# A convolution kernel in fp32: GpSimd's products released by their pixels alone, and three steps of the start in another order

## What is computed

```python
t1 = p1_w * x                          # a factor per channel and row
t2 = x + t1
t4 = relu(x)
t5 = unfold(x, 3, 7)                   # the 21 taps of a 3 x 7 window
t7 = einsum('oc,nchw->nohw', p7_w, t4)
t8 = unfold(t7, 1, 5, dilation 3)      # five columns, three apart
t9 = x[:, :, None] - t8
t10 = einsum('ngihw,goi->ngohw', t2 in 4 groups, p10_w in 4 groups)
t11 = einsum('nck,nmk->ncm', t1, t5) / sqrt(h * w)
t12 = t9.mean(2)
t13 = einsum('ncm,nmk->nck', t11, t10) / sqrt(c * 21)
out = maximum(t13, t12)
```

## Time and profile before

| what | value |
|---|---|
| time, median of 3 runs | 389.67 us (389.62 to 389.78) |
| the profiled execution | 390.18 us |
| its span, first to last instruction | 388.4 us |
| mean granted clock of TensorE, as a share of 2.4 GHz | 0.999 |
| TensorE busy with matmuls | 381.5 us |
| VectorE busy | 328.2 us |
| ScalarE busy | 254.2 us |
| GpSimd busy | 88.7 us |
| data moved by DMA | 88.8 MB, mean 229 GB/s |

### The profile page before, as it was taken

The page is one execution under the profiler, slowest core; times in us unless marked ns, Lnnn a source line. Parts: engine busy times, 40 slices in busy tenths (PEclk is TensorE's granted clock), DMA queues, the critical chain, the costliest instruction groups (busy, mean ns, idle before and its releaser), DMA issues.

```text
span 388.4 us, 10235 instructions
## 1 busy us (share of the span) xinstructions
PE 381.5 (98%) x4024; PEld 169.4 (44%) x4024; DVE 328.2 (85%) x401; ACT 254.2 (65%) x721; POOL 88.7 (23%) x77
## 2 busy tenths in 40 slices
PE   6999999999999999999999999999999999999996
PEld 3233563334733356333643338333383334732383
DVE  7898999899798896888968887888868889688645
ACT  2535379779577664677466772776827768377790
POOL 1635212221232202222022220222202222222300
PEclk9999999999999999999999999999999999999999
DMA  7999486483977656784677937779377673553115
GB/s 281 388 350 410 181 283 210 167 303 114 328 268 258 212 199 218 257 308 147 215 223 259 337 112 248 232 265 322 120 250 249 246 283 111 174 181 111 54 57 216
DMA packets 28704, 88.80 MB, mean 229 GB/s; under 512 B 3312, under 2 KB 3824, under 8 KB 28656
## 3 DMA queue, kind: packets, MB, share of 16 engines
q1 hardware_dynamic: 28656, 88.14, 65.0%
HBM read 71.35 MB, written 16.78 MB: 227 GB/s over the span
## 4 chain that ended last, share of the span: by engine, by line
PE 98%; issue 1%; DVE 0%; DVEq 0%
PE ps_y L828 43%; PE ps_y L927 13%; PE ps_t L850 12%; PE ps_p L850 12%; PE ps_y L839 9%; PE ps_t L927 2%; PE ps_y L850 1%; PE ps_y L1072 1%; PE ps_p L1010 1%; PE ps_t L828 1%; PE ps_y L975 1%; PE ps_p L828 1%; PE ps_p L975 0%; PE ps_t L1010 0%; PE ps_t L839 0%
## 5 line engine op out<-in xcount | busy, mean ns | idle before, releaser
L828 PE MATMUL ps_y<-v_planes,u_planes 64*64 64x512 f32 x1488 | 183.4, 594 | 2.0 <-issue 1.8
L306 POOL TENSOR_TENSOR t1T<-t1T,p1T_sb 128x512 f32<-128x512 f32 x64 | 81.2, 1292 | 267.8 <-PE ps_y L839 237.0
L414 ACT ACTIVATE t<-xn,p_plus 128x64 f32<-128x64 f32 x512 | 127.9, 334 | 0.0
L850 PE MATMUL ps_t<-t,aT 64*64 64x512 f32 x440 | 113.0, 590 | 0.1
L850 PE MATMUL ps_p<-box,p_fifth 64*64 64x512 f32 x424 | 108.8, 589 | 0.0
L828 PEld LDWEIGHTS ps_y<-v_planes,u_planes 64*64 64x64 f32 x1488 | 54.9, 133 | 112.9 <-issue 107.9
L641 DVE STREAM_TRANSPOSE yT<-ps_y 128x512 f32<-128x512 f32 x62 | 40.7, 695 | 30.3 <-PE ps_y L839 29.9
L338 ACT ACTIVATE base<-ps_p 128x512 f32<-128x512 f32 x55 | 32.8, 597 | 47.4 <-PE ps_p L850 46.9
L927 PEld LDWEIGHTS ps_y<-t1T,yT 128*128 128x128 f32 x448 | 50.5, 192 | 5.7 <-issue 5.7
L927 PE MATMUL ps_y<-t1T,yT 128*128 128x128 f32 x448 | 51.9, 277 | 0.0
L675 DVE TENSOR_TENSOR base<-ps_t,base 128x512 f32<-128x512 f32 x56 | 38.5, 687 | 12.0 <-PE ps_t L850 11.8
(11 more groups left out here) (75 smaller groups left out, 219.1 us busy)
## 6 DMA issues: line engine op xcount, KB each, us to landing
xw<-x_conv SPq DMA_DIRECT2D x63, 561.0 KB, 6.6
xn<-x_nat SPq DMA_DIRECT2D x32, 512.0 KB, 4.5
t1T<-x_pix SPq DMA_DIRECT2D x32, 512.0 KB, 5.1
out<-base SPq DMA_DIRECT2D x63, 256.0 KB, 4.7
u_planes<-w_tiles SPq DMA_DIRECT2D x4, 336.0 KB, 6.4
out<-base SPq DMA_DIRECT2D x2, 128.0 KB, 2.1
p1T_sb<-p1T SPq DMA_DIRECT2D x1, 128.0 KB, 7.4
p_sb<-p7T SPq DMA_DIRECT2D x1, 64.0 KB, 7.7
```

The lines of the kernel that those rows point to most:

```text
L306: nc.gpsimd.tensor_tensor(part, part, p1T_sb[:, e, :].unsqueeze(1).broadcast_to([P, 4, C]), ALU.mult).then_inc(t1_ready, 1)
L414: last = nc.scalar.activation(t2[:, h, W * r:W * (r + 1)], xn[:, f, at:at + W], ACT.Copy, scale=p1_plus[:, 8 * h + r:8 * h + r + 1])
L828: last = nc.tensor.matmul(dst[TILE * pair:TILE * pair + TILE, :], weights_of(rows_of(half), u, weights, TILE * k, TILE), data_of(rows_of(h ...
L850: last = nc.tensor.matmul(dst[cols, 0:data.shape[-1]], weights[rows, cols], data[rows, :], start=start, stop=False, skip_group_check=True)
```

## The change

It has three parts.

GpSimd's parts of t1 no longer wait for `m_done` in images 1 to 7. What stays is the wait for the quarter of pixels that they read. Image 0 keeps both.

In the start, x of group 5 (the sixth) is loaded ahead of quarters 2 and 3 of image 0's pixels and of the second natural tile.

Also in the start, VectorE does `box_pairs(0, 0)` ahead of the planes of group 5 instead of behind `seeds(4)`, and ScalarE does `t2_half(0, 1)` behind two `seed_x` instead of ahead of `copy_two(4)`.

```diff
             load_group(4)
+            load_group(5)
             load_pixels(0, 2, 4)
             load_natural(0, 1)
-            load_group(5)
             load_natural(0, 2)
...
             for n in range(1, N_IMG):
-
                 for q in range(8):
-                    pool.wait_ge(m_done, GROUPS * n + 1 + q // 2)
                     t1_part(n, q)
...
             relu(0, 1)
-            t2_half(0, 1)
 
             copy_two(4)
             seed_x(0, 0)
             seed_x(0, 1)
+            t2_half(0, 1)
...
             seeds(3)
+            box_pairs(0, 0)
             planes_low(5)
             planes_high(5)
             turn_y(2)
 
             seeds(4)
-            box_sums(0, 0)
+            box_fours(0, 0)
+            box_last(0, 0)
```

## The result

The changed kernel takes 413.47 us in the median, against 389.7: the ratio is 1.0596, 95% interval 1.0569 to 1.0623, so 23.8 us slower. Six executions lie between 410.18 and 417.14 us; those of before agree within 0.2 us. The ratio is taken without the slowest one, 417.14, which lies over 1.5% above the fastest. The profiled execution took 412.30 us, its span is 410.5.

The account below looks back on a forecast made before the run. TensorE, busy 381.5 of 388.4 us, was taken as the bound. Images 2 to 7 lose 13.5 and image 1 4.8, the start and tail 0: 18.3 us on 389.67 gives 408.0 us, range 391 to 420.

Parts of the forecast that it names:

- narrower range: Whole kernel: the range of the turns case alone, 401 to 414 us, within the wider 391 to 420.
- the bound with 1.25 for each part: Images 1 to 7: GpSimd parts taken at 1.25 us instead of 1.12, five meetings an image; loss 22.9 us, not 18.3.
- The bound: From 46 us to the tail TensorE waits for nobody; delaying another engine costs only what exceeds its slack.
- the fall of the clock: Rival: TensorE's clock drops to 1.2 GHz after each stall for as long, adding half of 18.3; 417 us, chance 0.07.
- Taking turns: GpSimd and VectorE alternate whole instructions on shared SBUF ports; later images' planes and boxes wait, image 3 stalls 2.4 us; chance 0.60.
- The rivals of one engine that keeps its turn over a run of operations: Shared SBUF ports: VectorE keeps them, 391 to 400 us, chance 0.13; GpSimd keeps them, 428 us, chance 0.08.
- Only operations with two SBUF inputs: VectorE's planes and box sums meet GpSimd; `turn_y`, `seeds` and `max_half` read PSUM and keep their lengths.
- The slack: Second max before the t13 product: first 1.7 us of added VectorE time free in later images, 0.55 in image 1.
- Images 2 to 7: Slot after `y_times_t1`: TensorE stalls behind the second max, 2.0 to 2.6 us an image, 13.5 us together.
- Image 1: Less slack there: meetings add 5.5 us to VectorE, the second max ends late, TensorE loses 4.8 us.
- The start: First microseconds, reordered loads, box operation and t2 half: 0 us; 0.4 to 1 us at most if the cover fails.
- The collision of the last plane with GpSimd's third pair: Start, image 0: last plane meets GpSimd's parts, `turn_y(2)` comes about one, maybe two microseconds later; no cost to TensorE.

Follow-up runs that it names:

- half-size parts: Against the kernel before: wait removed in images 1 to 7, each GpSimd eighth done as two operations of 128x256 instead of one of 128x512; 394.1 us, ratio 1.0108.
- half of the parts: Against the kernel before: wait removed for parts 0 to 3 of images 1 to 7, kept for parts 4 to 7; 391.34 us, ratio 1.0041.
- its move: Against the kernel before: wait removed in images 1 to 7, second max put ahead of `box_pairs` in images 2 to 7; 406.15 us, ratio 1.0428.
- the start alone: Against the changed kernel: the wait for `m_done` put back, so only the new order of the start remains; 389.71 us, ratio 1.0001 to the kernel before.

## Why the prediction was right, and where it was not

It said slower, 408.0 us with a range of 391 to 420; it is 413.5. Its narrower range had a slip: the bound with 1.25 for each part gives 389.67 + 22.9 = 412.6, not 414.

**The bound** held: in images 2 to 7 the period of the changed kernel's chain is that of before plus the stall, to 0.1 us; in image 1 the fall of the clock comes on top.

**Taking turns** held, with its durations. The working put the end of `box_pairs` of image 3 at 162.9; it ended at 171.63, which is 162.9 on the old time scale (less 8.75). The stall was worked out at 2.4 and is 2.5. That a VectorE operation waits for one part and no more was open, since parts have no wait between them: it is shown by the 1.79 and 1.80 of the planes, and by the half-size parts. The rivals of one engine that keeps its turn over a run of operations are excluded by the same rows: GpSimd's eight parts took 13.99 us, five of VectorE's operations came between them.

**Only operations with two SBUF inputs** held: among 56 records of the max in the changed kernel none is longer than 0.69.

**The slack** held: 1.2 us of added waits were called free, and half of the parts (0.9 us of waits in image 3) cost nothing from image 3 on. That the second max is what TensorE meets first is shown by its move.

**Images 2 to 7**: 13.5 was forecast, 15.6 came. About half of the difference is `box_last`. Images 5 and 6 were put at 2.0 each and took 2.6 and 2.7: I had moved part 2 ahead of `box_last` with the early landing of before's trace, and `box_last` took 1.74 and 1.87 there, so it waited 0.5 and 0.65 where I had 0.2. In image 4 (2.6 forecast, 3.0 measured) it took 2.19. The other half is some 0.15 us in every image. Image 3 shows it: `box_last` ended 0.1 sooner than forecast, and the stall was longer all the same, since from there to the end of `box_pairs` it took 8.04 us (forecast 7.97) and the product started 0.14 us behind the end of the max, where the working had 0.05.

**Image 1** is the step that failed in size: 4.8 forecast, 7.1 to 7.6 measured in the four profiles in which it has the long stall. The stall itself is 4.5 to 4.7 us, so the sum of the meetings was nearly right, but in part by luck. In the changed kernel's profile part 0 didn't delay `box_fours` (0.9 forecast) and `box_last` waited 0.2 instead of 0.85; in their place the next `box_fours`, which the working didn't have, met the last part and took 2.17 instead of 1.22. The rest, 2.6 to 2.9 us, is the fall of the clock, which the prediction had as a rival of its own with 0.07, instead of a term of the sum. It was a term: it came in each of these four profiles, and behind single short waits as well. What the prediction named against it, 1.8 us without work before the first data at full clock, was a single case; the runs have both outcomes at this length. Without the clock the profiled execution would have lost 4.5 + 15.6 = 20.1 us, where 18.3 was forecast. The clock also explains most of the 7 us by which the changed kernel scatters: the execution with the highest, 0.995, took 410.18 us, the one with the lowest, 0.983, took 417.14, and the missing 1.2% of the span is 5 us (an estimate).

**The start**: 0, and it is 0 within the 1.1 us that the measurement can tell (389.71). In the changed kernel the box operation runs at 31.37, the planes from 32.60, the sum plane ends at 34.52, TensorE takes it at 35.74. The working had a slack of 0.6; it came out at 1.2. TensorE and VectorE both stood 0.6 us sooner in this execution, which leaves the slack as it is; but in before the first plane and the second each began some 0.2 us later behind the operation ahead of them than here, and the working had kept that. The collision of the last plane with GpSimd's third pair was forecast and happened neither in this profile nor in that of the start alone; it did in the five profiles in which x of group 5 came latest (planes begun at 32.99 or later, the last one up to 1.80).

## What to carry to other kernels

A wait that looks superfluous can be a time table: here it kept GpSimd beside VectorE's PSUM work, where they don't meet. Before removing such a wait, list which instructions of the other engine will now run beside the freed ones, and compare the added waits with the slack of the first consumer behind them; below it they are free (1.6 us for half of the parts), above it every one is paid (24 us for all). If the burst must come, shorter instructions halve the price of each meeting (the burst itself took 17.28 us instead of 13.99), and the consumer's operation belongs ahead of those that wait (8 us of the 24 came back). No version here was faster than the kernel before.

## What the runs showed of the hardware that I had not expected

TensorE's granted clock fell to 0.50 at waits of 3.5 to 3.7 us every time (four profiles). At shorter ones it fell three times, at 1.79, 1.88 and 2.08 us, and stayed at 1.00 at others as long or longer: 1.83, 1.84, 1.85, 2.00, 2.01 and 2.75. By the stretches of 2 us (an estimate) a fall lasted 3.4 us behind the short waits and 6.8 at the long ones; it cost 1.7 us and 2.6 to 2.9 us beyond the stall. Two of the three behind short waits began only 0.9 and 1.4 us after TensorE had work again. What decides at the short ones stays open.

Meetings chain. In the start a load that came 1 to 2 us late moved a plane onto a GpSimd part (1.80 for 0.72), the delay moved a box operation onto the next (2.17 for 1.22), and TensorE stood for the last of them.

After the stall of image 3 two products of an output pair, which start 0.02 us apart in the steady state (160.02 and 160.04), were recorded some 0.1 us apart for the rest of the slot (177.44 and 177.55); that this costs time is not shown, since the periods grew by no more than the stalls.
